# Cutting the weight casts into pieces, triple-buffering the wmod slices and reordering the first transfers

## The reference

```python
mod = (silu(c) @ wmod).reshape(8, 6, 1, 1024)          # wmod is [1024, 6144]
sa, ca, ga, sb, cb, gb = (mod[:, i] for i in range(6)) # ga, gb pushed to |g| >= 0.25
h = layernorm(x) * (1 + ca) + sa
q, k, v = h @ W_q.T, h @ W_k.T, h @ W_v.T              # 16 heads of 64
attn = (q @ k.T) * decay / 8                           # decay = gamma_h ** (t - s), causal
y = group_norm(attn @ v)                               # per head over time and width
x = x + ga * (y @ W_o.T)
h = layernorm(x) * (1 + cb) + sb
s = h @ Win + bin
g = sum_j relu(s * W1_j + b1_j) * W2_j + b2            # 64 units, 16 each
x = x + gb * (g @ Wout + bout)
```

## Time and profile before

| | us |
|---|---|
| time before, median of 2 runs | 1005.53 (1004.31 to 1006.76) |
| the profiled execution's own time | 1009.25 |
| span of its slowest core, core 3 | 1007.7 |
| spans of the eight cores | 992.0 to 1007.7 |

### The profile page before, as it was taken

The page is one execution under the profiler, slowest core; times in us unless marked ns, Lnnn a source line. Parts: engine busy times, 40 slices in busy tenths (PEclk is TensorE's granted clock), DMA queues, the critical chain, the costliest instruction groups (busy, mean ns, idle before and its releaser), DMA issues.

```text
span 1007.7 us, 8211 instructions; the slowest of 8 cores (992.0 to 1007.7 us)
## 1 busy us (share of the span) xinstructions
PE 487.5 (48%) x2518; PEld 211.0 (21%) x2518; DVE 394.1 (39%) x677; ACT 215.2 (21%) x339; POOL 42.5 (4%) x74
## 2 busy tenths in 40 slices
PE   0000221176764575777778784444545454444541
PEld 0000000033322232333343342111111111111110
DVE  0000012235556654566666653433333333333332
ACT  1000001122322313144435310022112111121121
POOL 6000000000000000000000000000000000000000
PEclk9999755588776887777888895756566666555555
DMA  7999999925543235123222320011112212111121
GB/s 100 111 112 103 164 152 157 155 49 95 95 87 71 49 78 94 32 57 63 61 53 53 74 53 1 11 52 53 52 54 72 65 62 59 55 53 52 53 73 32
DMA packets 124123, 73.35 MB, mean 73 GB/s; under 512 B 105022, under 2 KB 117360, under 8 KB 123824
## 3 DMA queue, kind: packets, MB, share of 16 engines
q0 software_dynamic: 20400, 39.26, 23.1%
q1 hardware_dynamic: 103680, 33.57, 17.8%
HBM read 60.62 MB, written 16.78 MB: 77 GB/s over the span
## 4 chain that ended last, share of the span: by engine, by line
DVE 32%; PE 19%; SPq 16%; DMA 13%; issue 9%; ACT 8%; POOL 1%; DVEq 1%; ACTq 0%; POOLq 0%
SPq L410 16%; PE ps L507 9%; DVE sqs L187 7%; DVE h L187 7%; DMA kfm<-ktm 5%; DMA hT<-h 5%; ACT qtm L727 5%; DVE st L187 4%; DMA wsc<-wq 3%; DVE ktm L187 2%; DVE x L187 2%; DVE xa L187 2%; PE psY L643 2%; PE psY L645 2%; DVE ysumc L187 2%
## 5 line engine op out<-in xcount | busy, mean ns | idle before, releaser
L613 PE MATMUL ps<-wt_o,ybf 128*128 128x512 bf16 x256 | 91.8, 523 | 49.0 <-DVE x L187 42.2
L463 PE MATMUL ps<-wmsl,silb_sb 128*1 128x512 bf16 x96 | 37.5, 561 | 160.0 <-DMA wmsl<-wmod 145.8
L187 DVE SCALAR_TENSOR_TENSOR xa<-psY,x 128x1024 f32<-128x1024 f32 x16 | 19.6, 1224 | 190.0 <-PE psY L645 190.0
L507 PE MATMUL ps<-wt_q,hT 128*128 128x512 bf16 x256 | 82.6, 494 | 17.3 <-DMA hT<-h 17.3
L727 ACT ACTIVATE qtm<-psS,b1pp_sb,wp_sb 128x128 bf16<-128x128 f32 x128 | 46.4, 468 | 120.2 <-PE psS L627 120.2
L507 PE MATMUL ps<-wt_k,hT 128*128 128x512 bf16 x256 | 61.2, 395 | 10.8 <-DVE qtm L187 10.8
L187 DVE CAST mrow_sb<-ps 1x512 bf16<-1x512 f32 x12 | 8.1, 679 | 134.9 <-PE ps L463 134.1
L507 PE MATMUL ps<-wt_v,hT 128*128 128x512 bf16 x256 | 59.3, 379 | 0.0
L627 PE MATMUL psS<-hT,windup 128*128 128x128 bf16 x128 | 15.9, 302 | 89.2 <-DMA hT<-h 89.2
L187 DVE TENSOR_TENSOR st<-psS,mask_sb 128x512 bf16<-128x512 f32 x64 | 44.3, 692 | 36.4 <-PE psS L531 30.8
L678 ACT ACT_TABLE_LOAD x16 | 20.5, 1283 | 158.4 <-DVE var L187 158.4
(11 more groups left out here) (126 smaller groups left out, 628.3 us busy)
## 6 DMA issues: line engine op xcount, KB each, us to landing
xa<-x POOLq DMA_DIRECT2D x32, 512.0 KB, 3.6
wmsl<-wmod POOLq DMA_DIRECT2D x12, 1024.0 KB, 12.2
out<-xa SPq DMA_DIRECT2D x16, 512.0 KB, 2.6
wsc<-wq POOLq DMA_DIRECT2D x1, 2048.0 KB, 27.9
wsc<-wk POOLq DMA_DIRECT2D x1, 2048.0 KB, 46.8
wsc<-wv POOLq DMA_DIRECT2D x1, 2048.0 KB, 65.5
wsc<-wo POOLq DMA_DIRECT2D x1, 2048.0 KB, 82.2
mask_sb<-c_mask POOLq DMA_DIRECT2D x1, 512.0 KB, 5.1
```

The lines of the kernel that those rows point to most:

```text
L187: ins = getattr(v, name)(*a, **kw)
L463: mm2 = t.matmul(ps4[0:1, :], silb_sb[:, dc:dc + 1], wmsl[:, 512 * dc:512 * (dc + 1)], start=(dc == 0), stop=(dc == NDC - 1))
L507: mm = t.matmul(ps01[:, 512 * hf:512 * (hf + 1)], hT[p][:, 128 * dc:128 * (dc + 1)], wt[nm][:, 1024 * dc + 512 * hf:1024 * dc + 512 * (hf ...
L613: t.matmul(ps01[:, 512 * hf:512 * (hf + 1)], ybf[:, 1024 * tau + 128 * dj:1024 * tau + 128 * (dj + 1)], wt["o"][:, 1024 * dj + 512 * hf:10 ...
```

## The change

- The four casts are cut into eight pieces of 128 rows; a piece is issued when the piece before it has landed (`wcast`). Each transposing DMA of SP waits for its own piece only.
- The wmod slices rotate through three buffers (`wmv`): `wmsl` and the columns 8192 to 12287 and 12288 to 16383 of `ybf`, which chunks 8 to 15 fill much later. Slice s waits until slice s - 1 has landed and until gemv s - 3 is done. ScalarE waits for gemvs 11 and 12 before it writes Y of chunks 8 and 12.
- POOL's order is slices 0, 1, cast q, slices 2, 3, cast k, slices 4, 5, cast v, slices 6, 7, cast o, slices 8 to 11.
- The x loads of the loop are issued by ScalarE: tiles 0 and 1 behind silu, tile 2 ahead of the loop, tile c + 3 at the head of chunk c.
- SP's order is wq, hT(0), wk, qT(0), wv, kT(0), hT(1), wo, qT(1), kT(1), then hT, qT, kT of each chunk.
- In chunk 0 TensorE waits for wq, wk and wv each ahead of its own groups.

```diff
--- before.py
+++ after.py
@@ -160,6 +160,12 @@
     ps4 = nc.alloc_psum_tensor("ps4", [128, 512], F32)
     psY = nc.alloc_psum_tensor("psY", [128, 1024], F32)
     ps7 = nc.alloc_psum_tensor("ps7", [128, 512], F32)
+
+    def wmv(s):
+        r = s % 3
+        if r == 0:
+            return wmsl, 0
+        return ybf, 8192 + 4096 * (r - 1)
 
     sem_names = [
         "s_cst", "s_wc0", "s_wc1", "s_wc2", "s_wc3",
@@ -403,13 +409,14 @@
             def chain():
                 pass
 
-            for i, nm in enumerate(("q", "k", "v", "o")):
-                s.wait_ge(S[f"s_wc{i}"], 16)
+            def wts(i, nm):
                 for oc in range(8):
+                    s.wait_ge(S[f"s_wc{i}"], 16 * (oc + 1))
                     dst = wt[nm][:].rearrange("p (dj oc b) -> p dj oc b", dj=8, oc=8)[:, :, oc, :]
                     s.dma_start_transpose(dst, wsc[i][128 * oc:128 * (oc + 1), :]).then_inc(
                         S[f"s_wt{nm}"], 16)
-            for c in range(KB_NCH):
+
+            def hT_tr(c):
                 p = c % 2
                 s.wait_ge(S["vp"], vpos[("h", c)])
                 if c >= 2:
@@ -417,18 +424,37 @@
                 s.dma_start_transpose(
                     hT[p][:].rearrange("p (dj b) -> p dj b", dj=8), htl[p][:]
                 ).then_inc(S[f"s_hT{p}"], 16)
-                if KB_STAGE < 2:
-                    continue
+
+            def qT_tr(c):
+                p = c % 2
                 s.wait_ge(S["vp"], vpos[("qe", c, 1)])
                 if c >= 2:
                     s.wait_ge(S["t_Y"], c - 1)
                 s.dma_start_transpose(
                     qfm[p][:].rearrange("p (dj b) -> p dj b", dj=8), qtm[p][:]
                 ).then_inc(S[f"s_qT{p}"], 16)
+
+            def kT_tr(c):
+                p = c % 2
                 s.wait_ge(S["vp"], vpos[("qke", c)])
                 s.dma_start_transpose(
                     kfm[p][:].rearrange("p (dj b) -> p dj b", dj=8), ktm[p][:]
                 ).then_inc(S[f"s_kT{p}"], 16)
+
+            wts(0, "q")
+            hT_tr(0)
+            wts(1, "k")
+            qT_tr(0)
+            wts(2, "v")
+            kT_tr(0)
+            hT_tr(1)
+            wts(3, "o")
+            qT_tr(1)
+            kT_tr(1)
+            for c in range(2, KB_NCH):
+                hT_tr(c)
+                qT_tr(c)
+                kT_tr(c)
             if not KB_PH3:
                 return
             for tau in range(NCH):
@@ -459,9 +485,10 @@
                     t.wait_ge(S["vp"], vpos[("modp", s - 1)])
                 if s == 11:
                     t.wait_ge(S["vp"], vpos["bfh0"])
+                wten, wbase = wmv(s)
                 for dc in range(NDC):
                     mm2 = t.matmul(ps4[0:1, :], silb_sb[:, dc:dc + 1],
-                                   wmsl[:, 512 * dc:512 * (dc + 1)],
+                                   wten[:, wbase + 512 * dc:wbase + 512 * (dc + 1)],
                                    start=(dc == 0), stop=(dc == NDC - 1))
                 mm2.then_inc(S["t_gemv"], 1)
                 t.wait_ge(S["vp"], vpos[("mrow", s)])
@@ -487,9 +514,6 @@
                     t.matmul(ps4[0:1, 0:512], b2b_sb[:, 0:1],
                              wout_sb[0:64, 512:1024], start=True,
                              stop=True).then_inc(S["t_bf"], 1)
-                if c == 0:
-                    for nm in ("q", "k", "v"):
-                        t.wait_ge(S[f"s_wt{nm}"], 16 * 8)
                 t.wait_ge(S[f"s_hT{p}"], 16 * (c // 2 + 1))
                 for g, (nm, hf) in enumerate(
                         (("q", 0), ("q", 1), ("k", 0), ("k", 1), ("v", 0), ("v", 1))):
@@ -503,6 +527,8 @@
                         t.wait_ge(S["vp"], vpos[("qke", c)])
                     else:
                         t.wait_ge(S["vp"], vpos[("qe", c, g - 2)])
+                    if c == 0 and g in (0, 2, 4):
+                        t.wait_ge(S[f"s_wt{nm}"], 16 * 8)
                     for dc in range(NDC):
                         mm = t.matmul(
                             ps01[:, 512 * hf:512 * (hf + 1)],
@@ -657,6 +683,12 @@
             sc.wait_ge(S["s_cst"], NC_ALL)
             sc.activation(silf_sb[:], cfm_sb[:], AF.Silu).then_inc(S["sc_silu"], 1)
 
+            def x_load(c):
+                if c >= 2:
+                    sc.wait_ge(S["vp"], vpos[("hA", c - 2)])
+                sc.dma_start(xa[c % 2][:], x_d[128 * c:128 * (c + 1), :]).then_inc(
+                    S[f"s_xa{c % 2}"], 16)
+
             def sc_tab(c):
                 p = c % 2
                 if c >= 2:
@@ -678,14 +710,19 @@
                 sc.activation(rho[:, c:c + 1], var[:, c:c + 1], AF.Sqrt,
                               bias=actb_sb[:, 1:2], scale=1.0).then_inc(S["sc_rho"], 1)
 
+            x_load(0)
+            x_load(1)
             sc_tab(0)
             sc_sq(0)
             sc_rho(0)
             sc_tab(1)
             sc_sq(1)
             sc_rho(1)
+            x_load(2)
             for c in range(KB_NCH):
                 p = c % 2
+                if c + 3 < KB_NCH:
+                    x_load(c + 3)
                 if c + 2 < KB_NCH:
                     sc_sq(c + 2)
                     sc_tab(c + 2)
@@ -697,6 +734,10 @@
                 sc.copy(vtm[p][:, 512:1024], ps01[:, 512:1024]).then_inc(S["sc_ve"], 1)
                 if c + 2 < KB_NCH:
                     sc_rho(c + 2)
+                if c == 8:
+                    sc.wait_ge(S["t_gemv"], 11)
+                if c == 12:
+                    sc.wait_ge(S["t_gemv"], 12)
                 sc.wait_ge(S["t_Y"], c + 1)
                 sc.copy(ybf[:, 1024 * c:1024 * (c + 1)], psY[:]).then_inc(S["sc_ye"], 1)
                 if c >= 1:
@@ -764,32 +805,35 @@
                 win_d[:, :].rearrange("(c p) m -> p c m", c=NDC),
             ).then_inc(S["s_cst"], 16)
 
-            for i, wd in enumerate((wq_d, wk_d, wv_d, wo_d)):
-                g.dma_start(wsc[i][:, :], wd[:, :]).then_inc(S[f"s_wc{i}"], 16)
-
             def wm_load(s):
                 j = SLICE_ORDER[s]
                 if s >= 1:
-                    g.wait_ge(S["t_gemv"], s)
+                    g.wait_ge(S["s_wm0"], 16 * s)
+                if s >= 3:
+                    g.wait_ge(S["t_gemv"], s - 2)
+                wten, wbase = wmv(s)
                 g.dma_start(
-                    wmsl[:].rearrange("p (c o) -> p c o", c=NDC),
+                    wten[:, wbase:wbase + 4096].rearrange("p (c o) -> p c o", c=NDC),
                     wmod_d[:, :].rearrange("(c p) o -> p c o", c=NDC)[:, :, 512 * j:512 * (j + 1)],
                 ).then_inc(S["s_wm0"], 16)
 
-            def x_load(c):
-                if c >= 2:
-                    g.wait_ge(S["vp"], vpos[("hA", c - 2)])
-                g.dma_start(xa[c % 2][:], x_d[128 * c:128 * (c + 1), :]).then_inc(
-                    S[f"s_xa{c % 2}"], 16)
+            def wcast(i, wd):
+                for oc in range(8):
+                    if oc >= 1:
+                        g.wait_ge(S[f"s_wc{i}"], 16 * oc)
+                    g.dma_start(wsc[i][128 * oc:128 * (oc + 1), :],
+                                wd[128 * oc:128 * (oc + 1), :]).then_inc(S[f"s_wc{i}"], 16)
 
             wm_load(0); wm_load(1)
-            x_load(0)
+            wcast(0, wq_d)
             wm_load(2); wm_load(3)
-            x_load(1)
-            for c in range(2, NCH):
-                if c + 2 < 12:
-                    wm_load(c + 2)
-                x_load(c)
+            wcast(1, wk_d)
+            wm_load(4); wm_load(5)
+            wcast(2, wv_d)
+            wm_load(6); wm_load(7)
+            wcast(3, wo_d)
+            for s_i in range(8, 12):
+                wm_load(s_i)
             if KB_PH3:
                 for tau in range(NCH):
                     if tau <= 1:
```

## The result

The changed kernel takes 1037.26 us in the median (1032.49 to 1043.37), the kernel before, on the same chips, 1009.24: a ratio of 1.0287, 95% interval 1.0256 to 1.0317. It is 28 us slower, and lies 1 us outside the range of 980 to 1036. The forecast of 1008 stood on a kernel before of 1005.53 us; that kernel measured 3.7 us more here. The other 26 of the 29 us between forecast and result are the sum's.

A forecast was written before the change was run, and what follows sets the result against it. The start was taken as bound by transfers, afterwards by POOL's latency chain. Chunk 0's 20 us gain was lost behind wo's transposes, kT(1) 2.4 us late: 1007.7 + 2.4 = 1010.1, on the median's scale 1008 us; range 980 to 1036.

The forecast's parts named there:

- x on ScalarE: x loads moved to ScalarE's queue, costed at nothing; without cover by its idle time they would cost 4.6 us.
- A piece spreads over all the engines: Assumption behind the piece price; on half the engines a piece costs 2.65 us more, total 1093, chance 0.06.
- the price of a piece, 4.65 us: One 128-row cast piece on POOL's queue: gap 0.6, fixed part 2.05, moving 2.0 us; bounds 4.1 and 5.2.
- The 25 periods in the chain: Piece periods in POOL's chain of the start: six in each of three blocks, seven in the last, at 4.65 us.
- the 247.1 predicted: Landing of kT(1), issued at 240.8 behind wo's transposes on SP; 2.4 us later than in the kernel before.
- the gain in chunk 0: S(0) was to come near 197 us instead of 217.4, 20 us early, then lost again in chunk 1.
- slice 0: First wmod slice on POOL, following the constants: 22.4 + 6.9, landing at 29.3 us.
- the four blocks' slice with piece 0: Start of each weight's block on POOL: a slice and the first piece together, 0.6 + 10.4 + 2.0 = 13.0 us.
- piece 7 with the next slice: Between POOL's blocks: a weight's last piece and the slice behind it, 11.55 us plus 2 for transposes, 13.55.
- from o7 to kT(1): From the landing of wo's last piece, at 238.2, through SP's order to kT(1) landing at 247.1.
- run in the 2.6 us in which nothing of POOL's is moving: Weight transposes, about 1.3 us each, were to fit between POOL's pieces and add nothing to a piece.
- the second rival, transposes inside the chain: Transposes go ahead of POOL's next piece: up to 5.95 us a piece, 25 x 1.3 = 32, 1040; chance 0.13.

The follow-up runs named there:

- r1_wo_late: The changed kernel with SP's eight transposes of wo moved from between hT(1) and qT(1) to behind hT(3): ratio 1.0070 to the kernel before.
- r2_hold: The changed kernel, but SP issues a weight's eight transposes only when all eight pieces of it have landed: ratio 1.0300 to the kernel before.
- r3_whole: The changed kernel with each cast whole again, one DMA a weight, the new order and three slice buffers kept: ratio 1.0089 to the kernel before.
- r6_first_hold: Against r3_whole: slices 0 to 3, then all four whole casts; weight transposes start only when all casts landed, wo's behind hT(3): ratio 0.9994 to the kernel before.
- r11_four_late_slices: r9_four_late with only slice 4 ahead of the v pieces, slice 5 ahead of the o pieces, slices 6 to 11 behind all casts: 0.9859 to the kernel before.
- r9_four_late: r8_four_pieces with wo's transposes moved behind hT(3) on SP: ratio 0.9890 to the kernel before.
- r8_four_pieces: The changed kernel with four pieces of 256 rows for each weight instead of eight of 128: ratio 0.9975 to the kernel before.
- r7_first_nohold: r6_first_hold, but each weight's transposes may start as soon as its own cast has landed: ratio 0.9970 to the kernel before.
- r12_whole_small: r11_four_late_slices with whole casts, one DMA a weight, cut by the DMA into 4 KB runs: ratio 0.9955 to the kernel before.

## Why the prediction was wrong

**Right.** The start is what the change moves, and POOL's chain is its path (64% and 20% in the chain of waits). SP does stand in wo's transposes behind chunk 0, qT(1) and kT(1) come right behind them, S(1) waits for them (28.9 us), and the rest is as long as before (761.7 against 763.0). r1_wo_late proves that link: moving wo's transposes gave 22 us back. x on ScalarE costs nothing (1.0004). A piece spreads over all the engines, as assumed: the six pieces of r2_hold's row are 192 packets on q0, 32 a piece, of which 16 carry the 256 KB written, 16 KB each, and 16 are closing ones of under 512 B. That is how the Trainium skill describes the split of a contiguous copy ("DMA: Bandwidth & Descriptors", section "Why a DMA increments its semaphore by 16 and not by 1").

**Wrong: the price of a piece, 4.65 us.** The 25 periods in the chain took 142.2 us (wq 34.6 for six, wk 37.5, wv 33.2, wo 36.9 for seven): 5.69 each. 25 x 1.04 = 26 us, and kT(1) landed 25.9 us after the 247.1 predicted. The same error takes away the gain in chunk 0: the 18 periods of wq, wk and wv took 105.3 us, not 83.7, and S(0) came at 219.1, not near 197. The other terms came even, and this is luck: slice 0 landed at 29.6 (29.3 predicted), the four blocks' slice with piece 0 took 14.1, 11.9, 10.4 and 11.5 us, 4.1 less than four times 13.0, piece 7 with the next slice 13.9, 12.6 and 14.3 (13.55 each), and from o7 to kT(1) 12.6 (8.9), 3.7 more.

The step that failed is the one sentence that let the transposes "run in the 2.6 us in which nothing of POOL's is moving". r2_hold took the transposes out of their own weight's pieces: a piece of the chain then costs 4.76 us on its slowest core and 4.68 on core 1, where the changed kernel has 5.69. So the sum for a piece without transposes was right, and the transposes, put at nothing, cost 1.0 us a piece, which is the error of 1.04 but for rounding. (In wq alone, with nothing else about, a piece takes 4.07, so 4.65 is right only as the mean of the chain.) They are released by the same landing as the next piece, and SP is the quicker: the first piece of wq lands at 43.7, SP issues its transpose at 43.8, POOL the next piece at 44.3. This is the second rival, transposes inside the chain, given 1.3 us a piece, 1040 us and a chance of 0.13. It deserved more: the earlier trace rows showed slices 1.8 us slower in the median wherever transposes were about. I set against it that a whole cast leaves a transpose standing for 56 us; there three more casts were queued ahead, each of 64 data packets, four for each engine (r3_whole has 704 packets less on q0 than the changed kernel: 28 DMAs of 16 closing ones, and 256 with data, so 256 for four casts). It says nothing of a piece of one packet for each engine that is issued last.

**A mistake the experiments brought out.** I took the start for a sum of POOL's latencies and expected 0.945 and 0.97 from r3_whole and r6_first_hold, which take the latencies away. Both came out beside the kernel before. With the chain of waits gone, transposes set the pace, and they run at less than half their pace beside slices (24.3 us for eight against 11.4 alone) and stand beside casts. In the kernel before, too, 82% of the start's chain was SP's transposes; its SP timeline reads

```profile
41.94 78.12 SPq L410 DMA_TRANSPOSE wt_q<-wsc  x8
120.18 22.67 SPq L410 DMA_TRANSPOSE wt_k<-wsc  x8
142.95 22.23 SPq L410 DMA_TRANSPOSE wt_v<-wsc  x8
165.28 35.42 SPq L410 DMA_TRANSPOSE wt_o<-wsc  x8
```

I read these 82% as waiting for casts. That holds for the 56 us up to 99.7; the other 101 us are 30 transposes at 3.4 us each, more than twice their pace alone. What wins is between the two: pieces of 256 rows, few waits, and nothing of wo ahead of chunk 1.

**Open.** Why a transpose beside other traffic is so slow is not shown; that it isn't the descriptors' size alone is. That the transpose reaches the DMA engines ahead of the next piece is read from the order of issue; only its price is measured. Why r11_four_late_slices gains nothing sure over r9_four_late is open too.

## What to carry to other kernels

When a transfer is cut into pieces that wait for one another, price a piece with what the same landing releases beside it: it wants the same engines and may be issued first. Multiply by the number of pieces before taking a term for small; 1 us of error was 26 here. And when part of a start comes earlier, look in every in-order queue for what now stands between it and the next chunk: in r8_four_pieces kT(0) came 29 us sooner than in the kernel before, and that could not pass eight transposes of a weight that is needed in chunk 3.

## What the runs showed of the hardware

- A casting copy of 512 KB (256 KB written), alone, lands 3.4 to 3.8 us after its issue (r2_hold, core 3; up to 4.0 on the others). The Trainium skill's fit ("DMA: Bandwidth & Descriptors", section "Anatomy of one DMA — SWDGE (gpsimd) path") gives an estimate of 3.2, close. With a transpose beside it 4.4 to 6.5 were measured (the changed kernel, core 1), which the fit for a single transfer does not cover.
- A transposing DMA of 128 x 1024 bf16 takes about 1.4 us when only its like are in flight (11.4 us for eight, r6_first_hold); beside slices about 3 us (24.3 and 25.7 for eight). Beside the three whole casts still queued two took 66 us to land (r7_first_nohold); beside casts in 4 KB runs eight took 71.6 us (r12_whole_small).
- From a landing to POOL's next issue pass 0.45 to 0.6 us, to SP's about 0.1.
